# An mLSTM and FP4 feed-forward kernel whose input and context rows are turned by VectorE in 32x32 blocks

## The reference

```
x = x + xattn(layernorm(x), ctx, ctx, ...)
x = x + ffn(layernorm(x), w_gate, w_up, w_down)

xattn: gates   ig, fg = [q, k, v] @ igate_w.T + b, [q, k, v] @ fgate_w.T + b
       D       = exp(log_D - rowmax(log_D)), log_D from cumsum(log_sigmoid(fg)) and ig, lower triangle
       C       = (q @ k.T / 8) * D          per head
       h       = C @ v / (normalizer + 1e-6), then a norm per head
ffn:   fp4_linear(x, w) = quant_dequant(x) @ quant_dequant(w).T
       y       = fp4_linear(silu(gate) * up, w_down)
```

## Time and profile before

| | before |
|---|---|
| time, median of 3 runs | 1805.06 us (1804.82 to 1805.08) |
| profiled execution, its time | 1805.26 us |
| its span, first to last instruction | 1803.5 us |
| mean granted TensorE clock | 0.982 |

### The profile page before, as it was taken

One profiled execution on the slowest core, in us unless ns is written; L12 is line 12 of the kernel. 1 busy time (PEld: TensorE's weight loads), 2 busy tenths in 40 slices (PEclk: granted clock), 3 DMA queues, 4 the chain that ended last, 5 costly groups with the idle time before them and its releaser, 6 DMA issues.

```text
span 1803.5 us, 41839 instructions
## 1 busy us (share of the span) xinstructions
PE 1728.7 (96%) x14073; PEld 948.2 (53%) x14073; DVE 1643.1 (91%) x3341; ACT 1363.7 (76%) x2810; POOL 1255.6 (70%) x1188
## 2 busy tenths in 40 slices
PE   4568999999999999999999999999999999999997
PEld 2444555555555555555555555555555555555553
DVE  8999989898998989899898989989898998989995
ACT  7787887777777777777777777777787777777653
POOL 7877767676766767676676767667676776767662
PEclk9579999999999999999999999999999999999999
DMA  6444454454544445344444545444444444544432
GB/s 206 136 106 117 120 127 111 111 137 100 133 115 122 114 111 137 100 130 118 114 118 116 130 107 128 121 108 124 116 127 110 122 126 104 128 104 110 102 68 62
DMA packets 342134, 211.77 MB, mean 117 GB/s; under 512 B 275200, under 2 KB 281856, under 8 KB 341920
## 3 DMA queue, kind: packets, MB, share of 16 engines
q1 hardware_dynamic: 341920, 209.10, 45.7%
HBM read 125.93 MB, written 17.30 MB: 79 GB/s over the span
## 4 chain that ended last, share of the span: by engine, by line
PE 89%; issue 1%; DVE 0%; DMA 0%; POOL 0%; ACT 0%; DVEq 0%; POOLq 0%
PE bank L480 49%; PE bank L607 9%; PE bank L608 8%; PE bank L609 8%; PE bank L578 4%; PE bank L496 4%; PE bank L571 2%; PE bank L590 2%; PE bank L541 1%; PE bank L508 1%; PE bank L520 1%; PE bank L551 0%; PE bank L458 0%; DMA xqT<-xqs 0%; DMA work<-stage 0%
## 5 line engine op out<-in xcount | busy, mean ns | idle before, releaser
L480 PE MATMUL bank<-wgTh,xqT 128*128 128x512 f16 (+1 forms) x1536 | 556.2, 362 | 3.9 <-DMA xqT<-xqs 2.9
L480 PE MATMUL bank<-wuTh,xqT 128*128 128x512 f16 (+1 forms) x1536 | 555.6, 362 | 0.0
L1055 POOL TENSOR_TENSOR stage<-stage,hs 128x512 f32<-128x512 f32 (+1 forms) x192 | 273.5, 1424 | 82.6 <-DVE stage L1263 82.6
L480 PE MATMUL bank<-wgTl,xqT 128*128 128x512 f16 (+1 forms) x768 | 278.0, 362 | 0.0
L480 PE MATMUL bank<-wuTl,xqT 128*128 128x512 f16 (+1 forms) x768 | 277.9, 362 | 0.0
L607 PE MATMUL bank<-wdTh,work 128*128 128x512 f16 x704 | 268.1, 381 | 7.0 <-DMA work<-stage 7.0
L608 PE MATMUL bank<-wdTl,work 128*128 128x512 f16 x704 | 267.3, 380 | 0.0
L609 PE MATMUL bank<-wdTh,work 128*128 128x512 f16 x704 | 267.3, 380 | 0.0
L480 PEld LDWEIGHTS bank<-wgTh,xqT 128*128 128x128 f16 x1536 | 151.1, 98 | 157.8 <-issue 8.5
L480 PEld LDWEIGHTS bank<-wuTh,xqT 128*128 128x128 f16 x1536 | 150.5, 98 | 141.7 <-issue 0.7
L1093 POOL TENSOR_TENSOR xn<-xn,xs 128x512 f32<-128x512 f32 x64 | 83.4, 1303 | 188.7 <-DVE xn L1329 188.7
(11 more groups left out here) (206 smaller groups left out, 3783.3 us busy)
## 6 DMA issues: line engine op xcount, KB each, us to landing
mb<-max_dram SPq DMA_DIRECT2D x64, 512.0 KB, 3.7
x<-in_x_dram SPq DMA_DIRECT2D x64, 256.0 KB, 3.3
cf<-in_ctx_dram SPq DMA_DIRECT2D x64, 256.0 KB, 4.0
cn<-in_ctx_dram SPq DMA_DIRECT2D x64, 256.0 KB, 3.3
wb<-warp_dram SPq DMA_DIRECT2D x128, 128.0 KB, 2.9
out_dram<-ob SPq DMA_DIRECT2D x64, 256.0 KB, 3.0
xb<-in_x_dram SPq DMA_DIRECT2D x60, 256.0 KB, 2.7
work<-stage SPq DMA_TRANSPOSE x192, 3.1
```

Of the source, the lines that this page charges most:

```text
L480: i = e.matmul(o[:, 0:width], x, w[:, c, n0:n0 + width], start=first and k < 2, stop=last and k >= 4)
L1055: e.tensor_tensor(blocks(hx[:, n0:n0 + w]), blocks(hx[:, n0:n0 + w]), per_block(hs2[:, n0 // BLOCK:(n0 + w) // BLOCK]), ALU.mult).then_inc ...
```

## The change

From tile 9 on (`blocked(t)`, 55 of the 64 tiles) neither row block goes through PE, PSUM and ACT. VectorE's `transpose` turns each 32x32 block of a 128x512 operand by itself, so the blocks have to be put in their right places before, and DMAs do that: the blocks of 32 values in a row (128 bytes) are the unit of the copy.

- Context: `sp_c_in` loads `cf` in four DMAs, of 32 partitions each, straight from the input in pieces of 128 bytes. `dve_cT` turns it into `cT`.
- x: ACT normalizes one turn sooner than before (`act_xh` of tile u in turn u, with the factor 0.125 put into the layer norm's scale). `sp_xh_out` writes `xb` to a DRAM buffer `xh_dram` of two slots, `sp_xz_in` reads it back in four DMAs in 128-byte pieces into the new tile `xzb`, and `dve_xT` turns that into `xT`. The sum and the square of the layer norm are done one turn sooner as well, and `xb` is refilled as soon as `xh_out` has landed.
- All five lists of a turn, and the lists of the start, are in a new order. `pe_u` now waits for `s_C[0]` ahead of its first matmuls.

```
+        def blocked(t):
+            return t.first >= 9
...
-            e.wait_ge(S_["x_T"], t.done(1))
+            if not blocked(t.back(1)):
+                e.wait_ge(S_["x_T"], t.done(1))
+            else:
+                e.wait_ge(S_["xh_out"], 16 * (t.first - 9))
             e.dma_start(xb[:, :], x_rows[tokens(t), :]).then_inc(S_["x_in"], 16)
 
+        def sp_xh_out(e, t):
+            e.wait_ge(S_["xh"], t.done())
+            if t.has(11):
+                e.wait_ge(S_["xz_in"], 64 * (t.first - 10))
+            e.dma_start(xh_dram[t.parity], xb[:, :]).then_inc(S_["xh_out"], 16)
+
+        def sp_xz_in(e, t):
+            e.wait_ge(S_["xh_out"], 16 * (t.first - 8))
+            if t.has(10):
+                e.wait_ge(S_["xT"], t.done(1))
+            rows = xh_dram[t.parity].rearrange("(q s) (k g f) -> g s k q f", s=SQ, g=P // SQ, f=SQ)
+            for g in range(P // SQ):
+                e.dma_start(xzb[g * SQ:(g + 1) * SQ, :].rearrange("s (k q f) -> s k q f", k=EC, f=SQ), rows[g]).then_inc(S_["xz_in"], 16)
...
+            e.wait_ge(S_["cT"], t.done(1))
+            rows = c_rows[tokens(t), :].rearrange("(q s) (k g f) -> g s k q f", s=SQ, g=P // SQ, f=SQ)
+            for g in range(P // SQ):
+                e.dma_start(cf[g * SQ:(g + 1) * SQ, :].rearrange("s (k q f) -> s k q f", k=EC, f=SQ), rows[g]).then_inc(S_["cz_in"], 16)
...
             e.wait_ge(S_["xw"], t.done())
+            e.wait_ge(s_C[0], t.done())
...
-            if t1.live(NT):
-                pe_x_T(e, t1)
-                pe_c_T(e, t1)
...
+        def dve_xT(e, t):
+            e.wait_ge(S_["xz_in"], 64 * (t.first - 8))
...
+            e.wait_ge(S_["xw"], t.done(8))
+            e.wait_ge(S_["qk"], t.done(8))
+            e.transpose(xT[:, t.slot, :, :].rearrange("p c s -> p (c s)"), xzb[:, :]).then_inc(S_["xT"], 1)
```

More of the change, by code:

```diff
@@ L124, in mlstm_fp4_ffn @@
         cf = sb("cf", [P, E])
+        xzb = sb("xzb", [P, E])
         junk = sb("junk", [P, E], BF16); junk2 = sb("junk2", [P, E], BF16)
@@ L558, in pe_u @@
             if later.live(NT):
-                e.wait_ge(S_["xT"], later.done())
+                if not blocked(later):
+                    e.wait_ge(S_["xT"], later.done())
                 if later.at_start(7):
@@ L582, in pe_st_mm @@
             later = t.back(-5)
-            if later.live(NT):
+            if later.live(NT) and not blocked(later):
                 e.wait_ge(S_["cT"], later.done())
@@ L678, in pe_start @@
+            pe_gu(e, T[1], 1); pe_row_T(e, T[7]); pe_c_T(e, T[8]); pe_gu(e, T[1], 2); pe_down(e, T[0], 0); pe_u(e, T[3]); pe_st_mm(e, T[3]); pe_down(e, T[0], 1)
             pe_down(e, T[0], 2); pe_qk(e, T[4])
@@ L818, in act_xh @@
             e.wait_ge(S_["ln1"], t.of(4, 2))
-            if t.has(1):
+            if t.has(1) and not blocked(t.back(1)):
                 e.wait_ge(S_["x_T"], t.done(1))
@@ L1182, in pool_turn @@
             if t6.live(NT):
-                pool_xw(e, t6)
+                pool_mask(e, t6, 1)
             if t7.live(NT):
@@ new lines, in pool_start @@
+            pool_w_qs(e, 2, 9); pool_w_qs(e, 2, 10); pool_un(e, T[2]); pool_mask(e, T[3], 0); pool_ln1_rs(e, T[8]); pool_ln1_nb(e, T[8]); pool_hx(e, T[0], 2)
+            pool_hx(e, T[0], 0); pool_mask(e, T[3], 1); pool_hx(e, T[0], 1); pool_sch(e, T[2]); pool_h_qs(e, T[0], 0); pool_rs2(e, T[2]); pool_h_qs(e, T[0], 1)
+            pool_ln1_rs(e, T[9]); pool_ln1_nb(e, T[9]); pool_h_qs(e, T[0], 2); pool_vc(e, T[3]); pool_xw(e, T[3]); pool_vk(e, T[3]); pool_x_qs(e, T[2])
+            pool_un(e, T[3]); pool_sch(e, T[3]); pool_hx(e, T[1], 1); pool_ln1_rs(e, T[10]); pool_ln1_nb(e, T[10])
@@ new lines, in dve_start @@
+            dve_w_lo(e, 1, 9); dve_w_pw(e, 2); dve_w_lo(e, 1, 10); dve_C(e, T[1], 1); dve_hn(e, T[0]); dve_w_t(e, 2, 0); dve_x1(e, T[0]); dve_w_q(e, 2, 0)
+            dve_w_t(e, 2, 1); dve_w_ws(e, 2); dve_w_q(e, 2, 1); dve_St(e, T[1]); dve_sd2(e, T[0]); dve_xam(e, T[0]); dve_xt(e, T[0]); dve_xi(e, T[0])
+            dve_w_t(e, 2, 2); dve_xn(e, T[0]); dve_xs(e, T[0]); dve_nr_neg(e, T[1]); dve_w_q(e, 2, 2); dve_x_t(e, T[0]); dve_nr(e, T[1]); dve_x_q(e, T[0])
+            dve_nq(e, T[1]); dve_C(e, T[2], 1); dve_n2(e, T[1]); dve_x_lo(e, T[0]); dve_vr(e, T[1]); dve_ve(e, T[1]); dve_w_lo(e, 2, 0); dve_w_t(e, 2, 3)
@@ new lines, in dve_start @@
+            dve_h_t(e, T[0], 0); dve_hs2(e, T[0]); dve_h_q(e, T[0], 0); dve_hn(e, T[2]); dve_h(e, T[1], 0); dve_x1(e, T[2]); dve_h_t(e, T[0], 2); dve_osc(e, T[0])
+            dve_h_lo(e, T[0], 0); dve_h_t(e, T[0], 1); dve_h_q(e, T[0], 1); dve_ham(e, T[1], 0); dve_xam(e, T[2]); dve_h_q(e, T[0], 2); dve_sd2(e, T[2])
+            dve_xt(e, T[2]); dve_h(e, T[1], 1); dve_h_lo(e, T[0], 1); dve_h_lo(e, T[0], 2); dve_xi(e, T[2]); dve_h(e, T[1], 2); dve_xn(e, T[2])
+            dve_ham(e, T[1], 1); dve_x_t(e, T[2]); dve_xs(e, T[2]); dve_ham(e, T[1], 2); dve_x_q(e, T[2]); dve_nr_neg(e, T[3]); dve_vr(e, T[3]); dve_nr(e, T[3])
```

381 lines of the change are left out of this document (191 added, 190 removed).

## The result

| | before | after |
|---|---|---|
| time, median | 1805.07 us (1804.82 to 1805.46, 4 runs) | 1759.37 us (1757.04 to 1760.9, 4 runs) |
| ratio | | 0.9747, 95% interval 0.9735 to 0.9759 |
| span of the profiled execution | 1803.5 us | 1759.1 us |
| mean granted TensorE clock | 0.982 | 0.980 |

The change makes the kernel 45.7 us faster. The forecast was 1762.0. One execution of the kernel before, measured beside e1 to e4, took 5259.66 us and is left out of their ratios.

A forecast was written before the change was run, and what follows sets the result against it. PE, busy 105.51 of 105.51 us in four turns, was taken as the bound. The profiled 1805.26 - 48.1 (transposes off PE) + 5 (stalls) = 1762.2 us, the median 0.2 lower, 1762.0; range 1753 to 1803.

The forecast's parts named there:

- PE is the bound and loses 0.87 us a turn: PE stays the bound without its eight transposes a turn; 55 tiles gain 48.1 us; four turns take 102.0 us; chance 0.53.
- DVE's transposes at 0.60 us: Two new 128x512 transposes a turn on DVE, each priced like a one-operand pass, 0.60 us.
- The upper bound of 1.49: Upper price of a DVE transpose, from the slowest 128x512 pass; four turns would then need 110.9 us of DVE.
- DVE's need of 99.8 us: DVE's time for four turns: 103.8 us with the transposes, less 4 us gained by the new order.
- its room of 2.2 us: What DVE was expected to have to spare under PE's 102.0 us in four turns.
- ACT and POOL worth nothing by themselves: ACT loses two copies a turn and POOL nothing; both far from the bound, at 82.15 and 73.86 of 105.51 us.
- The rival, DVE the bound: Without gain from the order, DVE needs 103.8 us in four turns: 1781.7 us; chance 0.23 for DVE-bound but faster.
- DMA pieces at 19 ns, 4.9 us a turn, hidden: The 128-byte pieces of `cf` and `xzb`, 256 on each engine a turn; load 71 us of 102 in four turns.
- The rival of 53 ns: Pieces of `cf` and `xzb` over 53 ns make the DMA engines the bound, slower than before; 1910 us at 60; chance 0.10.
- The 19-fold rival: A strided copy pays per element, 19 times the transposing DMA: 23 us a load, time about 3590 us; chance 0.02.
- SP and the refill of `xb`: Seven more SP issues; lost refill cover stalls ACT, then DVE; 5 us in all with `pe_u`'s wait; slower case within 0.07.
- The start at 0 plus or minus 5: The start up to turn 9, reordered, loses and gains no step worth a price: 0, give or take 5 us.

The follow-up runs named there:

- e1: The changed kernel with eight 128x128 transposes of the identity put back on PE ahead of `pe_gu`'s second piece, read by nobody: 1805.79 us, ratio 1.0000 to the kernel before.
- e4: The changed kernel with DVE's and POOL's turn lists in the order of the kernel before, new steps put in: 1775.22 us, ratio 0.9834 to the kernel before.
- e2: The changed kernel with four 128x128 transposes of the identity put back on PE in a turn: 1783.01 us, ratio 0.988 to the kernel before.
- e6: The changed kernel with the context transpose done two more times a turn on DVE: 1760.33 us, ratio 0.9753 to the kernel before.
- e7: The changed kernel with the context transpose done four more times a turn on DVE: 1843.64 us, ratio 1.0216 to the kernel before.
- e8: The changed kernel with two extra 128-byte-piece copies of the context rows a turn, eight DMAs right behind the load of `cf`: 1929.1 us, ratio 1.069 to the kernel before.
- e9: The changed kernel with two extra 128-byte-piece copies of the context rows, eight DMAs issued last in SP's turn: 1783.44 us, ratio 0.989 to the kernel before.
- e10: The changed kernel with both reordering loads cut into 64-byte pieces and eight DMAs each: 1845.53 us, ratio 1.0242 to the kernel before.
- e11: The changed kernel with the context turned by DMA alone, `cf` loaded in 4-byte pieces by four DMAs and copied by DVE: 5200.8 us, one execution.
- e3: The changed kernel with `cf` and `xzb` loaded in whole 2 KB rows, not 128-byte pieces, blocks not reordered: 1759.01 us, ratio 0.9743 to the kernel before.

## Why the prediction was right, point by point

- **PE is the bound and loses 0.87 us a turn: right, and shown.** Four turns take 101.96 us (102.0 predicted). e1 and e2 put the transposes back, and the time comes back in proportion: 46.4 us for all of them (48.1 by the sum).
- **DVE's transposes at 0.60 us: right.** The rows have 0.62 and 0.63 from start to start. The upper bound of 1.49 was far off: that was a pass of two operands beside POOL, and a transpose isn't slowed there.
- **DVE's need of 99.8 us: close, but partly by luck.** The share at which it is full puts it at 99.0. The prediction gave the order 1 us a turn, by quicker 512-column passes over the hidden values and a quicker `dve_hn`. These became quick, as it said (678 and 692 ns, and `dve_hn` 627), but `dve_x1`, `dve_h_lo`, `dve_x_t` and `dve_xs` took over their collisions and used up the gain (2.16 against 2.21 us a turn). The prediction had warned only of `dve_x_t` and `dve_x_q`. The order paid all the same, by the two 384-column passes, 1.31 us a turn, which stand in no term of the prediction. And its room of 2.2 us was too small: e6 put 8 x 0.73 = 5.8 us more into four turns at no cost, since a collision gives its time back when the list moves along.
- **ACT and POOL worth nothing by themselves: right.** POOL did get lighter, though the prediction had it losing nothing: 66.91 us in four turns for 73.86, its passes over the hidden values 1121 ns for 1424 (the pages' rows for `pool_h_qs`). It isn't the bound, so nobody sees it.
- **The rival, DVE the bound: didn't happen.** It would take three or four more transposes a turn (e7). The new order (e4) is worth 15.9 us, near the 19.7 us between 1781.7 and 1762.0, but its loss shows as late feeds of `pe_down` and not as a full DVE, so the nearness is luck.
- **DMA pieces at 19 ns, 4.9 us a turn, hidden: the mechanism right, the term too dear.** They take 15 ns and 3.9 us (14 ns by e8, e9 and e10). In four turns the load is 64 us, for the 71 predicted. The rival of 53 ns: not near, at 128 and 64 bytes. The 19-fold rival: didn't happen at 128 bytes either; what a copy in single values costs, e11 shows.
- **SP and the refill of `xb`: right about the place, wrong about the price.** The sum of issues was one short (12 became 20), which changes nothing here. The five us for stalls (0.1 us a turn) weren't there: in 400 to 1600 us ACT waited for `xb` 1.4 us, in 3 places. But the cover is 1.5 us and no more, and e8 shows what it is worth if gone. This rival deserved a time of its own rather than a share in 7 in 100.
- **The start at 0 plus or minus 5: right.** It is 2.3 us longer (168.65 for 166.36 at tile 4's score product, the end of the start). From there the gain is 46.7 us; the 1.4 missing to 48.1 may be the first turns, where PE waits 2.9 us in all (160 to 400 us), 1.9 of it once in `pe_u` for `pool_xw`. That wasn't tested.
- **The sum.** 1805.26 - 48.1 + 2.3 + 1.4 = 1760.9, which is the profiled execution of the change (span 1759.1 and 1.8 around it). It has to come out, since 1.4 is what was left over. The prediction had 1762.2 for it, 1.3 more. It put 5 us on stalls and nothing on the start, and the record has 1.4 and 2.3, so two errors cancel in part. The main term, 48.1 us, doesn't depend on them.

## What to carry to other kernels

When the bound engine has work that another can do, price it by the starts of its neighbours, and then look at the issuing queue as closely as at the engine that takes the work: here DVE had 5.8 us of hidden room in four turns, and SP 1.5 us ahead of one load. The same DMAs cost 24 or 170 us by where they stood in SP's list, so a load that has to be prompt goes ahead of those that don't. An order written for one form of the kernel isn't neutral for another: the list of before, kept for the start, cost 11 us. And a pass that gets out of one collision may only hand it to the next: add up all groups of the engine before a new order is called cheaper.

## What the runs showed of the hardware

- A transpose of 128x512 in f32 on DVE takes 0.70 us, and 0.70 to 0.71 beside POOL's `pool_xw`; a pass on two SBUF operands that starts in the same place waits: 917.55 + 1.33 = 918.88, which is the end of `pool_xw` (917.06 + 1.27 = 918.33) and 0.55 more, what the same pass needs from its start to the next in e6 (919.91 to 920.45). `dve_xs`, over only 128x32 values, does the same beside `pool_h_qs`: it ends at 913.38 + 0.93 = 914.31, and that one at 913.22 + 1.05 = 914.27. By the Trainium skill, page SBUF — State Buffer, section SBUF: two separate sides, the ports that the two engines share are an exclusive lock, for DVE passes with two SBUF inputs among others; the rows of `dve_h_lo` agree.
- A DMA piece of 128 or of 64 bytes costs an engine 14 to 15 ns of busy time (e3, e8 to e10). With 4 bytes it is 8.7 ns of busy time, but one piece goes through every 16.3 ns (e11). The Trainium skill, page DMA: Bandwidth & Descriptors, section Specifications, says that transfers under 512 bytes miss line rate. That agrees: 128 bytes in 15 ns are 8.5 GB/s on an engine, and the 122 ns for 2 KB that the prediction read from the earlier trace rows are 16.8. Here the loss in a turn is 1.63 us of a DMA engine (e3), wholly hidden.
- SP's issue grows with the pieces: 0.67 us for 64 KB in 512 pieces of 128 bytes (2.69 / 4), 0.67 for 32 KB in 512 pieces of 64 bytes (5.40 / 8, e10), and 0.34 us for the 256 KB refill of `xb` in rows. With 4-byte pieces SP stood in its issues for 67 us (e11).
- In e11, where PE is busy for 35% of the span, the mean granted clock was 0.672, against 0.980 in the change.
